# Second attention of a four-layer network: score banks 3 to 4, first-pass banks 4 to 3, and two heads' matmuls issued in turn

## The chip, the cores and the metric

One core of a Trainium2 chip. The time is that of one execution on the device, in microseconds (us). PE is TensorE, DVE VectorE, ACT ScalarE, POOL GpSimd, SP SyncE.

## The reference, cut to what matters

Four layers over x of 2048 tokens with 128 features. Each adds an attention and a feed-forward block to x. The change is in the attention of layer 1, a causal one with 16 heads of 8 features and a relative-position bias:

```python
B, T, C = x.shape                  # in the kernel: 2 sequences of 1024 tokens
qkv = x @ W_attn + b_attn
att = jnp.einsum('bhtd,bhsd->bhts', q, k) * (1.0 / math.sqrt(D)) + rel_bias
att = jnp.where(causal, att, -jnp.inf)
att = jax.nn.softmax(att, axis=-1)
y = jnp.einsum('bhts,bhsd->bhtd', att, v)
return y.transpose(0, 2, 1, 3).reshape(B, T, C) @ W_proj + b_proj
```

## The kernel before

The function `attention_phase` runs twice, for layer 0 and, with `causal` true, for layer 1 (the "second attention", about 507 to 796 us of the trace). 2 x 16 heads make 8 quads of four heads, one turn of the loop each. Every quad is done in two passes.

The **first pass** finds the maximum of each query's scores. Its *units* are a query tile of 128 and up to 512 keys of one head: PE writes the scores to one bank of `mbank` (L821), adds the bias close to the diagonal (L829), and DVE reduces the bank to a negative maximum (L1025) and frees it. 48 units make a quad: 24 pairs, first for the even head (`jj` = 0), then for the odd one (`jj` = 1). Two more uses of the banks are transposes of the maxima ("late" and "turn", L794), which DVE splits into two parts (L1000, L1002); SP sends them back as rows (L560). L1030 combines the maxima once per quad. So 50 uses (`USES`) per quad, taken in turn by the `NM` banks of `mbank`.

The **second pass** goes through 12 groups, key tiles 0 to 3 for the first 512 queries, then 0 to 7 for the second 512; I call them groups 0 to 11. In a group PE writes the four heads' scores, one bank of `ebank` each (L850, three bias parts L859 near the diagonal), ACT takes the exponential (L982) and frees the bank, and PE multiplies all four by the values (L873, 8 matmuls in two passes of float32), one group later. ACT copies the result out (L972). The score banks are `NE`.

A head's operands lie in one half of the partitions: heads 0 and 2 of a quad in rows 0 to 63 of the array, heads 1 and 3 in rows 64 to 127. Each step writes the upper and lower 64 outputs by two matmuls. A plain L850 or L821 step is thus two matmuls of 64 by 64, which use half of the array's rows; the values use all.

PE issues in a fixed order. While quad q's second pass runs, the first pass of quad q + 1 is fed in between: `starts` says which units go with which group. `issue` takes steps of several generators in turn, one `yield` each. The waits that matter:

```python
pe.wait_ge(m_empty, q * USES + (use + 1))   # L812; m_empty starts at NM, +1 per reduction
pe.wait_ge(p_full, step + ...)              # in scores: NE exponentials back
pe.wait_ge(p_full, q * STEPS + (g * QUAD + QUAD + NE))   # in values: all four of the group
```

After the last quad's first pass, eight projection tiles (L429) take banks of `mbank`, one every five uses, and DVE adds them to x (L1092), behind its own work on the next weights.

Of the kernel before, what the change touches and what calls it, by code (L numbers as in the profile page):

```python
# [23 lines left out]
SEQ = 1024  # L24
# [15 lines left out]
NQUAD = BATCH * HEADS // QUAD  # L40
# [423 lines left out]
def attention_phase(nc, S, name, causal, loads=(), weights=None, sort=False):  # L464
# [19 lines left out]
    uses = units[:2] + ["late"] + units[2:18] + ["turn"] + units[18:]  # L484
    USES = len(uses)
    LATE, TURN = uses.index("late"), uses.index("turn")
    NM, WIDE = (4, 512) if causal else (2, SEQ)
    groups = [(h, kt) for h in range(2) for kt in range(4 * h + 4 if causal else BT)]
    lows = [max(kt * P - 512 * h, 0) if causal else 0 for h, kt in groups]
    starts = first_pass_starts(uses, groups, lows, causal)  # L490
    G = len(groups)
    opening = EARLY + starts[len(EARLY):] if causal else starts
    STEPS = QUAD * G
    NE = 3
    BQ = HEADS // QUAD
    layer = 1 if causal else 0
    tiles_from = NQUAD * USES + 1
# [5 lines left out]
    with nc.cleanup_on_exit(), ExitStack() as ctx:  # L503
# [22 lines left out]
        mbank = ctx.enter_context(nc.psum_tensor(f"{name}_mbank", [P, NM, WIDE], F32))  # L526
        ebank = ctx.enter_context(nc.psum_tensor(f"{name}_ebank", [P, NE, 512], F32))

# [37 lines left out]
        def _(sp):  # L566
# [78 lines left out]
            if sort:  # L645
                load_masks()
                sp.wait_ge(bias_parts, 4)
                sp.wait_ge(p_full, NE)
                for copy in range(BATCH):
# [137 lines left out]
        def _(pe):  # L787
            def transpose_maxima(n, units_done, quads_done, h):

                pe.wait_ge(m_empty, max(NM + units_done, n + 1))  # L790
                if quads_done and causal:
                    pe.wait_ge(combined, quads_done)
                bank = n % NM
                nc.tensor.transpose(mbank[0:2 * BT, bank, 0:P], negmax[:, h, :], S.ident[:]).then_inc(m_full, 1)  # L794
# [39 lines left out]
            def scores(q, g, j, buf):  # L834

                h, kt = groups[g]
                s = g * QUAD + j
                pr, jj = j // 2, j % 2
                if kt == 0:
                    pe.wait_ge(rows_loaded[h], q * 64 + 64)  # L840

                step = q * STEPS + s
                pe.wait_ge(p_full, step + (NE if s == 0 and (STEPS - 1) % NE == 0 else 1))
                lo = lows[g]
                rows, mine = slice(64 * jj, 64 * jj + BROWS), slice(64 * jj, 64 * (jj + 1))
                turn = S.anti[mine, 64 * (1 - jj):64 * (2 - jj)]
                near = causal and kt >= 4 * h - 1
                for c in range(P // COLS):
                    at = kt * P + COLS * c
                    last = nc.tensor.matmul(ebank[COLS * c:COLS * (c + 1), s % NE, lo:512],  # L850
                                            S.b_still[rows, buf, pr, at:at + COLS], S.b_moving[rows, buf, h, pr, lo:512],
                                            start=True, stop=not near)
                yield
                for part in range(PARTS if near else 0):
                    for c in range(2):
                        at = kt * P + HALF * c - 512 * h
                        first, end = max(at, 0), min(at + NEARBY, 512)
                        if first < end:
                            last = nc.tensor.matmul(ebank[HALF * c:HALF * (c + 1), s % NE, first:end], turn,  # L859
                                                    bias_b[mine, buf, pr, part, first - at:end - at],  # L860
                                                    start=False, stop=part == PARTS - 1)
                    yield
                last.then_inc(e_full, 1)

            def values(q, g, buf):

                h, kt = groups[g]
                if kt == 0:
                    pe.wait_ge(acc_empty, q * 2 + (h + 1))
                pe.wait_ge(p_full, q * STEPS + (g * QUAD + QUAD + NE))  # L870
                lo = lows[g]
# [6 lines left out]
            def issue(*steps):  # L878
                steps = list(steps)
                while steps:  # L880
                    steps = [s for s in steps if next(s, True) is None]

            def turn(q):

                buf = q % 2
                pe.wait_ge(b_loaded[buf], q // 2 * B_DMA + B_DMA)
                for g in range(G):
                    at = starts if q else opening
                    n, end = q * USES + at[g], q * USES + at[g + 1]
                    middle = (n + end) // 2  # L890
                    if causal:
                        issue(scores(q, g, 0, buf), scores(q, g, 1, buf))
                        issue(first_pass(n, middle))
                        issue(scores(q, g, 2, buf))
                        previous(q, g)
                        issue(scores(q, g, 3, buf))
                        issue(first_pass(middle, end))
                    else:
                        issue(scores(q, g, 0, buf))
                        issue(scores(q, g, 1, buf))  # L900
                        issue(first_pass(n, middle))
                        issue(scores(q, g, 2, buf))
                        previous(q, g)
                        issue(scores(q, g, 3, buf))
                        issue(first_pass(middle, end))

            def previous(q, g):
                if g:
                    values(q, g - 1, q % 2)
                elif q:  # L910
                    values(q - 1, G - 1, (q - 1) % 2)

            def first_pass(n, end):
                for n in range(n, end):
                    if n < NQUAD * USES:
                        yield from a_use(n // USES, n % USES)
                    elif n == NQUAD * USES:
                        transpose_maxima(n, n, NQUAD, 1)
                    elif n >= tiles_from and (n - tiles_from) % tile_every == 0 and (n - tiles_from) // tile_every < BT:
                        projected((n - tiles_from) // tile_every)  # L920
                        yield

            def projected(t):

                n = tiles_from + t
                pe.wait_ge(m_empty, NQUAD * USES + max(t + 2, NM + 1))
                pe.wait_ge(divided, 1)
                project_tile(nc, S, layer, t, mbank[:, n % NM, 0:P]).then_inc(m_full, 1)
# [10 lines left out]
            if sort:  # L939
                for side in range(2):  # L940
                    issue(first_pass(10 * side, 10 * side + 10))
                    bias_rows(side)
            issue(first_pass(20 if sort else 0, opening[0]))
            for q in range(NQUAD):
                turn(q)
            values(NQUAD - 1, G - 1, (NQUAD - 1) % 2)
# [1767 lines left out]
```

## Time and profile before

| | us |
|---|---|
| median of 3 runs | 1042.45 (1040.85 to 1044.25) |
| span of the profiled execution | 1041.8 |
| PE busy | 903.3 (87%) |
| DVE busy | 804.5 (77%) |
| ACT busy | 612.7 (59%) |
| second attention, first to last exponential | 524.6 to 794.4 |

### The profile page before, as it was taken

To read this page: it belongs to the slowest core of one execution; us is meant where nothing else is said; L and a number is where in the kernel's file an instruction comes from. 1 tells how busy PE (TensorE), PEld (TensorE's weight loads), DVE (VectorE), ACT (ScalarE), POOL (GpSimd) and SP (SyncE) were. 2 spreads that over 40 slices of the span, in tenths; PEclk is the share of its full clock that TensorE was granted. 3 is DMA by queue.
4 is the path that set the end of the run, shared out by engine and by line. 5 is a ranking of instruction groups with operands and counts; after the bars stand their busy time and mean duration, and the time that the engine had idled before them with its cause. 6 is when DMAs were issued, how large, how long until landed. Compare 5 with 4: busy or idle time off the path is not lost. (4 is left out here: it accounts for less than half of the span.)

```text
span 1041.8 us, 22164 instructions
## 1 busy us (share of the span) xinstructions
PE 903.3 (87%) x8501; PEld 460.0 (44%) x8501; DVE 804.5 (77%) x1600; ACT 612.7 (59%) x1280; POOL 199.4 (19%) x249
## 2 busy tenths in 40 slices
PE   5589999999999898975689999999989998777788
PEld 3212222222222223873345545555434776645568
DVE  7789999999899861647777878777851677799687
ACT  3228888888888686534146777676653446433552
POOL 2202033341202110540200001103000023123221
PEclk9659999999999899996679999999975998988899
DMA  2632435523426320111645544333100000000001
GB/s 77 189 82 65 113 101 117 117 56 90 110 83 130 116 39 15 53 50 41 191 104 144 151 103 103 86 82 89 42 6 23 12 1 2 1 0 1 4 6 36
DMA packets 62677, 73.71 MB, mean 71 GB/s; under 512 B 21143, under 2 KB 46864, under 8 KB 62558
## 3 DMA queue, kind: packets, MB, share of 16 engines
q1 hardware_dynamic: 48222, 49.23, 19.3%
q0 software_dynamic: 8576, 17.86, 7.0%
q10 hardware_dynamic: 5776, 5.22, 1.6%
q8 instruction: 68, 1.11, 0.5%
q14 instruction: 35, 0.29, 0.1%
HBM read 44.59 MB, written 18.16 MB: 60 GB/s over the span
## 5 line engine op out<-in xcount | busy, mean ns | idle before, releaser
L1025 DVE TENSOR_REDUCE a_negmax<-a_mbank 128x1 f32<-128x1024 f32 (+4 forms) x640 | 488.1, 817 | 73.8 <-PE a_mbank L829 36.0
L982 ACT ACTIVATE a_probs<-a_ebank 128x512 f32<-128x512 f32 (+3 forms) x896 | 436.2, 555 | 171.0 <-PE a_ebank L859 89.9
L850 PE MATMUL a_ebank<-b_moving,b_still 50*128 50x512 bf16 (+4 forms) x1280 | 270.7, 368 | 20.9 <-ACT a_probs L982 11.2
L821 PE MATMUL a_mbank<-a_moving,a_still 48*128 48x512 bf16 (+4 forms) x1280 | 262.8, 376 | 22.7 <-DVE a_negmax L989 10.0
L873 PE MATMUL a_acc<-a_probs,a_slot_v 128*32 128x512 f32 (+3 forms) x1792 | 226.9, 580 | 1.1 <-ACT a_probs L982 1.1
L850 PEld LDWEIGHTS a_ebank<-b_moving,b_still 58*64 58x64 bf16 (+1 forms) x1280 | 85.5, 102 | 257.0 <-ACT a_probs L982 200.6
L821 PEld LDWEIGHTS a_mbank<-a_moving,a_still 56*64 56x64 bf16 (+1 forms) x1280 | 69.0, 104 | 89.7 <-DVE a_negmax L1025 65.3
L859 PE MATMUL a_ebank<-a_bias_b,anti 64*64 64x176 bf16 (+4 forms) x1728 | 89.3, 233 | 0.0
L859 PEld LDWEIGHTS a_ebank<-a_bias_b,anti 64*64 64x64 bf16 x1728 | 70.6, 111 | 9.7 <-issue 1.5
L829 PE MATMUL a_mbank<-bias_a,anti 64*64 64x176 bf16 (+3 forms) x576 | 65.1, 237 | 0.0
L873 PEld LDWEIGHTS a_acc<-a_probs,a_slot_v 128*32 128x32 f32 x1792 | 35.8, 109 | 52.2 <-issue 41.0
L1501 DVE SCALAR_TENSOR_TENSOR x<-m_yp,w,x 128x128 f32<-128x128 f32 x128 | 36.0, 344 | 19.4 <-PE m_yp L1351 19.2
L436 POOL DMA_DIRECT2D sums<-vo x14 | 8.9, 639 | 206.1 <-ACT vo L972 164.9
L1190 ACT ACTIVATE m_hid<-m_hp,m_own 128x128 f32<-128x128 f32 x92 | 26.2, 368 | 27.8 <-PE m_hp L1149 27.8
L1351 PEld LDWEIGHTS m_yp<-w,m_hid 128*128 128x128 f32 x256 | 34.2, 196 | 18.8 <-issue 13.4
L1391 ACT ACTIVATE m_hid<-m_hp,b 128x512 f32<-128x512 f32 x32 | 21.5, 682 | 28.8 <-PE m_hp L1342 28.8
L1262 POOL DMA_INDIRECT spread_rows<-m_y,m_token x23 | 24.6, 1071 | 64.1 <-DVE m_y L1231 64.1
L1351 PE MATMUL m_yp<-w,m_hid 128*128 128x128 f32 x256 | 35.0, 281 | 2.2 <-ACT m_hid L1391 2.0
L1342 PE MATMUL m_hp<-xnT,w 128*128 128x512 f32 x64 | 35.1, 632 | 1.9 <-PEq L2651 1.9
L829 PEld LDWEIGHTS a_mbank<-bias_a,anti 64*64 64x64 bf16 x576 | 34.5, 113 | 2.8 <-issue 0.7
L1092 DVE TENSOR_TENSOR x<-a_mbank,x 128x128 f32<-128x128 f32 x16 | 4.3, 289 | 32.8 <-PE a_mbank L429 32.7
L1149 PE MATMUL m_hp<-m_xT,m_own 128*128 128x128 f32 x184 | 26.7, 291 | 1.6 <-DVE m_xT L1216 0.6
(388 smaller groups left out, 1116.3 us busy)
## 6 DMA issues: line engine op xcount, KB each, us to landing
a_slot_v<-vo SPq DMA_DIRECT2D x16, 512.0 KB
b_moving<-stack SPq DMA_DIRECT2D x64, 96.0 KB
b_still<-stack SPq DMA_DIRECT2D x32, 192.0 KB
a_still<-stack SPq DMA_DIRECT2D x60, 96.0 KB, 2.8
a_moving<-stack SPq DMA_DIRECT2D x60, 96.0 KB, 2.7
expert<-in_expert_rows POOLq DMA_DIRECT2D x8, 578.0 KB, 4.1
a_bias_b<-trow SPq DMA_DIRECT2D x32, 66.0 KB
b_moving<-a_mparts SPq DMA_DIRECT2D x124, 2.0 KB
```

The lines of the kernel that those rows point to most:

```text
L821: last = nc.tensor.matmul(mbank[COLS * c:COLS * (c + 1), bank, lo - left:hi - left], S.a_still[rows, q % 2, pr, at[c]:at[c] + COLS], S.a_m ...
L829: last = nc.tensor.matmul(mbank[COLS * c:COLS * (c + 1), bank, first - left:end - left], turn, bias_a[mine, q % 2, pr, first + shift:end + ...
L850: last = nc.tensor.matmul(ebank[COLS * c:COLS * (c + 1), s % NE, lo:512], S.b_still[rows, buf, pr, at:at + COLS], S.b_moving[rows, buf, h, ...
L859: last = nc.tensor.matmul(ebank[HALF * c:HALF * (c + 1), s % NE, first:end], turn, bias_b[mine, buf, pr, part, first - at:end - at], start ...
L873: last = nc.tensor.matmul(acc[32 * j:32 * (j + 1), lo:512], slot_v[:, buf, j, kt, :], probs[:, g % 2, j, lo:512], start=kt == 0, stop=g + ...
L982: nc.scalar.activation(probs[:, g % 2, j, lows[g]:512], ebank[:, s % NE, lows[g]:512], ACT.Exp).then_inc(p_full, 1)
L1025: nc.vector.tensor_reduce(to[:, at:at + 1], mbank[:, (index - 1) % NM, 0:right - left], AX.X, ALU.max, negate=True).then_inc(m_empty, 2 if ...
L1149: last = nc.tensor.matmul(hp[:, b % 2, m * P:(m + 1) * P], own[:, b % 3, m * P:(m + 1) * P], xT[:, b % 2, :], start=True, stop=True)
L1190: last = nc.scalar.activation(hid[:, b % 2, m, :], hp[:, b % 2, m * P:(m + 1) * P], ACT.Relu, bias=own[:, b % 3, MLP * P + m:MLP * P + m + 1])
L1342: nc.tensor.matmul(hp[:, i % HB, :], w1[:, e, :], S.xnT[:, c * CH:(c + 1) * CH], start=True, stop=True).then_inc(h_full, 1)
L1351: last = nc.tensor.matmul(yp[:, i % 2, t * P:(t + 1) * P], hid[:, i % 2, t * P:(t + 1) * P], w2[:, e, 0, :], start=True, stop=True)
L1501: last = nc.vector.scalar_tensor_tensor(S.x[:, CT * c + t, :], yp[:, i % 2, t * P:(t + 1) * P], w[:, CT * c + t, e:e + 1], S.x[:, CT * c + ...
```

## The change

For the causal attention only, `NM` goes from 4 to 3 banks of `mbank` and `NE` from 3 to 4 banks of `ebank`; the total stays at seven. In each group scores of heads 2 and 3 are issued together, step by step in turn, as heads 0 and 1 were, and ahead of the values of the group before instead of around them. `two_heads` issues two neighbouring units (even and odd head) in turn, and `whole` moves the borders of the groups so that no such pair is cut.

```diff
-    NM, WIDE = (4, 512) if causal else (2, SEQ)
+    NM, WIDE = (3, 512) if causal else (2, SEQ)
...
-    NE = 3
+    NE = 4 if causal else 3
...
                     if causal:
                         issue(scores(q, g, 0, buf), scores(q, g, 1, buf))
-                        issue(first_pass(n, middle))
-                        issue(scores(q, g, 2, buf))
+                        two_heads(whole(n), whole(middle))
+                        issue(scores(q, g, 2, buf), scores(q, g, 3, buf))
                         previous(q, g)
-                        issue(scores(q, g, 3, buf))
-                        issue(first_pass(middle, end))
+                        two_heads(whole(middle), whole(end))
...
+            def head_of_unit(n):
+                use = uses[n % USES]
+                return None if n >= NQUAD * USES or type(use) is str else use[3]
+
+            def whole(n):
+
+                return n + 1 if head_of_unit(n) == 1 else n
+
+            def two_heads(n, end):
+
+                while n < end:
+                    width = 2 if n + 1 < end and head_of_unit(n) == 0 else 1
+                    issue(*(first_pass(m, m + 1) for m in range(n, n + width)))
+                    n += width
...
-            issue(first_pass(20 if sort else 0, opening[0]))
+            if causal:
+                two_heads(0, whole(opening[0]))
+            else:
+                issue(first_pass(20, opening[0]))
```

What this moves on PE, first around group 6. These are PE's rows of the kernel before, from head 3's scores of group 5 (first row) to the values issued in group 6 (last row); x2 is one step of one head.

```order
L850 MATMUL a_ebank<-b_moving,b_still 64x512 x2
L821 MATMUL a_mbank<-a_moving,a_still 64x128 x2
L829 MATMUL a_mbank<-bias_a,anti 64x64
L829 MATMUL a_mbank<-bias_a,anti 64x128
L821 MATMUL a_mbank<-a_moving,a_still 64x512 x4
L850 MATMUL a_ebank<-b_moving,b_still 64x512 x4
L821 MATMUL a_mbank<-a_moving,a_still 64x256 x2
L829 MATMUL a_mbank<-bias_a,anti 64x176 x2
L821 MATMUL a_mbank<-a_moving,a_still 64x256 x2
L829 MATMUL a_mbank<-bias_a,anti 64x176 x2
L850 MATMUL a_ebank<-b_moving,b_still 64x512 x2
L873 MATMUL a_acc<-a_probs,a_slot_v 32x512 x4
```

The same place in the changed kernel, from the last units of group 5 to the units behind group 6's values:

```order
L821 MATMUL a_mbank<-a_moving,a_still 64x512 x4
L850 MATMUL a_ebank<-b_moving,b_still 64x512 x4
L821 MATMUL a_mbank<-a_moving,a_still 64x256 x4
L829 MATMUL a_mbank<-bias_a,anti 64x176 x4
L850 MATMUL a_ebank<-b_moving,b_still 64x512 x4
L873 MATMUL a_acc<-a_probs,a_slot_v 32x512 x4
L821 MATMUL a_mbank<-a_moving,a_still 64x512 x4
L821 MATMUL a_mbank<-a_moving,a_still 64x384 x4
L829 MATMUL a_mbank<-bias_a,anti 64x176 x4
```

Every unit now stands beside its twin (x4), the twin's L821 and its wait stand ahead of the first unit's bias L829, and all four scores stand ahead of the values.

The second place is the last quad's second pass, where only scores, values and projection tiles are left. PE before, from tile 3's group (the first row is the scores of group 4) to tile 5:

```order
L850 MATMUL a_ebank<-b_moving,b_still 64x512 x6
L873 MATMUL a_acc<-a_probs,a_slot_v 32x128 x4
L850 MATMUL a_ebank<-b_moving,b_still 64x512 x2
L429 MATMUL a_mbank<-heads_out,vo 128x128
L850 MATMUL a_ebank<-b_moving,b_still 64x512 x6
L873 MATMUL a_acc<-a_probs,a_slot_v 32x512 x4
L850 MATMUL a_ebank<-b_moving,b_still 64x512 x2
L429 MATMUL a_mbank<-heads_out,vo 128x128
```

And PE in the changed kernel, the same stretch:

```order
L850 MATMUL a_ebank<-b_moving,b_still 64x512 x8
L873 MATMUL a_acc<-a_probs,a_slot_v 32x128 x4
L429 MATMUL a_mbank<-heads_out,vo 128x128
L850 MATMUL a_ebank<-b_moving,b_still 64x512 x8
L873 MATMUL a_acc<-a_probs,a_slot_v 32x512 x4
L429 MATMUL a_mbank<-heads_out,vo 128x128
```

The scores of head 3 (x2) moved from between values and tile to ahead of the values; the tiles keep their groups.

## Rows read from the trace of the kernel before

**Rows 1.** The page, busy us, share of the span and instructions.
```profile
PE 903.3 (87%) x8501; PEld 460.0 (44%) x8501; DVE 804.5 (77%) x1600; ACT 612.7 (59%) x1280; POOL 199.4 (19%) x249
```

**Rows 2.** Line L1030: ns min/median/max, first and last start in us.
```profile
L1030 DVE TENSOR_TENSOR a_negmax<-a_negmax x8: 174/176/176, 534.4 to 751.4; 128x16 f32<-128x16 f32 x8
```

**Rows 3.** Windows: length, busy PE, PEld, DVE, ACT, POOL, granted clock, DMA, GB/s.
```profile
658.70:689.40 30.70, 29.34 (x578) 15.85 (x578) 24.58 (x53) 21.75 (x51) 2.62 (x5) 1.00 0.38 88
507.50:522.80 15.30, 12.76 (x109) 5.19 (x105) 15.01 (x34) 0.49 (x1) 3.73 (x1) 0.50 0.83 259
540.20:547.00 6.80, 6.80 (x60) 2.08 (x55) 3.77 (x9) 4.24 (x8) 0.00 (x0) 0.50 1.03 228
764.90:768.50 3.60, 0.10 (x2) 0.00 (x0) 3.43 (x7) 0.60 (x1) 0.00 (x0) 1.00 0.00 0
```

**Rows 4.** Waits of PE and DVE, 658.7 to 689.4: us, times, longest.
```profile
PE a_mbank L794 <- DVE a_negmax L1030: 0.7, 1, 0.7
PE a_mbank L794 <- DVE a_negmax L1025: 0.5, 1, 0.5
...
DVE a_negmax L1025 <- PE a_mbank L829: 4.3, 5, 1.3
DVE a_negmax L1025 <- PE a_mbank L821: 1.4, 3, 0.8
```

**Rows 5.** Lines by form, DVE, the same stretch: busy us, mean ns, idle before.
```profile
L1025 DVE TENSOR_REDUCE a_negmax<-a_mbank 128x1 f32<-128x512 f32 x24 | 15.2, 682 | 1.4 <-PE a_mbank L821 1.4
```

**Rows 6.** Timeline of DVE: start us, us of the merged run, xcount.
```profile
668.98 1.28 DVE L1025 TENSOR_REDUCE a_negmax<-a_mbank 128x1 f32<-128x512 f32 x2
...
658.82 0.48 DVE L1025 TENSOR_REDUCE a_negmax<-a_mbank 128x1 f32<-128x128 f32 x2
```

**Rows 7.** Timeline of PE behind head 3's scores of group 5.
```profile
670.79 0.44 PE L821 MATMUL a_mbank<-a_moving,a_still 56*64 56x512 bf16 x4
...
671.07 0.22 PE L829 MATMUL a_mbank<-bias_a,anti 64*64 64x64 bf16 x2
```

**Rows 8.** Timeline of PE in group 1, 384 columns.
```profile
659.25 0.36 PE L850 MATMUL a_ebank<-b_moving,b_still 58*64 58x384 bf16 x4
...
659.66 0.28 PE L821 MATMUL a_mbank<-a_moving,a_still 56*64 56x256 bf16 x4
...
659.85 0.33 PE L850 MATMUL a_ebank<-b_moving,b_still 58*64 58x384 bf16 x2
```

**Rows 9.** Timeline of PE around the values of group 6.
```profile
671.87 0.40 PE L850 MATMUL a_ebank<-b_moving,b_still 58*64 58x512 bf16 x2
672.20 1.06 PE L873 MATMUL a_acc<-a_probs,a_slot_v 128*32 128x512 f32 x8
...
673.20 0.61 PE L821 MATMUL a_mbank<-a_moving,a_still 56*64 56x512 bf16 x6
```

**Rows 10.** Timeline of DVE after the unit of 673.20.
```profile
673.69 1.75 DVE L1025 TENSOR_REDUCE a_negmax<-a_mbank 128x1 f32<-128x512 f32 x3 [0.21 <-PE a_mbank L821]
```

**Rows 11.** Timeline of all engines around one wait for a bank.
```profile
612.25 1.29 DVE L1025 TENSOR_REDUCE a_negmax<-a_mbank 128x1 f32<-128x512 f32 x2 [0.21 <-PE a_mbank L821]
...
612.99 0.10 PEld L821 LDWEIGHTS a_mbank<-a_moving,a_still 56*64 56x64 bf16 x2 [0.29 <-DVE a_negmax L1025]
613.00 0.40 PE L821 MATMUL a_mbank<-a_moving,a_still 56*64 56x512 bf16 x2
...
613.24 0.38 PE L850 MATMUL a_ebank<-b_moving,b_still 58*64 58x512 bf16 x2
```

**Rows 12.** Timeline of all engines at tile 4 of the last quad.
```profile
768.17 0.88 DVE L1092 TENSOR_TENSOR x<-a_mbank,x 128x128 f32<-128x128 f32 x4
...
768.51 0.49 PE L429 MATMUL a_mbank<-heads_out,vo 128*128 128x128 f32 x2 [3.51 <-DVE x L1092]
```

**Rows 13.** Timeline of PE in the last quad, at a clock of 0.50.
```profile
776.49 0.63 PE L850 MATMUL a_ebank<-b_moving,b_still 58*64 58x512 bf16 x2
...
777.33 0.79 PE L429 MATMUL a_mbank<-heads_out,vo 128*128 128x128 f32 x2
```

## The prediction

> **What bounds the kernel now.** The page's busy shares come first [rows 1]: PE 87%, DVE 77%, ACT 59%. They average many stages, so I cut the second attention out. L1030 runs once per quad, when the quad's first pass is done: 8 times from 534.4 to 751.4 us [rows 2], so an interval is 31.0 us in the mean, and the undisturbed one from 658.70 to 689.40 is 30.7 [rows 3]. In that stretch PE is marked busy for 29.3 us, DVE for 24.6, ACT for 21.8. PE waits 0.7 + 0.5 = 1.2 us for DVE, DVE waits 4.3 + 1.4 = 5.7 for PE [rows 4]. So PE bounds the quad and DVE is second, at about 25 us: no gain on PE can bring a quad below that.
>
> Two constants of DVE are needed later. A reduction of 512 columns takes 0.68 us [rows 5], but two take 1.28, so the next starts after 0.60; two of 128 take 0.48 [rows 6], so 0.28 long with a pitch of 0.20. Between the two I divide evenly: pitches 0.47 and 0.34 for 384 and 256 columns, lengths 0.55 and 0.42.
>
> **What is gained on PE.** A head uses one half of the array's rows. The obvious reading is that a step of one head leaves the other half idle. The trace says that part of this is used already. In the program the 128-column unit and its bias stand ahead of the 512-column units (the order is shown with the change), yet a 512-column L821 starts at 670.79 and the bias L829 of the 128-column unit only at 671.07 [rows 7]. Matmuls of different heads overtake each other. So I don't subtract idle halves; I add PE's steps up anew, with both heads at once:
> - Two heads' scores: with three bias parts at 384 columns, 659.25 to 659.66 = 0.41; a pair of units of 256 with bias, 659.66 to 659.85 = 0.19 [rows 8]; a plain step of 512, 613.00 to 613.24 = 0.24 [rows 11]. Scaled by columns, scores cost 0.45, 0.40, 0.34, 0.24 near the diagonal, 0.24 far from it and 0.34 at key tile 3, whose bias is short; two such pairs in each of 12 groups make 7.8 us. Units cost 0.30, 0.24, 0.18, 0.12 with bias (512 to 128 columns) and 0.24 without; 24 pairs make 5.3.
> - Values: 672.20 to 673.20 = 1.00, and the change-over ahead of it is 672.20 - 671.87 - 0.24 = 0.09 [rows 9], so 1.08 for 512 columns; two passes of 128 columns at 2.4 GHz are 0.11 and both heads' rows are needed, so each tile less takes 0.21 off. Six of 512 and two of each other width make 10.4.
> - Two transposes: 0.6.
> The sum is 24.1 us if PE never waits, against 30.7 - 1.2 = 29.5 now: **5.4 us to be had per quad**. ACT is no obstacle: with four score banks a head's scores wait for the exponential of the same head one group earlier, and ACT has 21.8 us of work in a quad. The copy L972 moves behind the values and still has a group's time.
>
> A page of the Trainium skill speaks against the overtaking: "TensorE: Matmul & The Clock Gate", Part 3, keeps matmuls in strict program order and lets only weight loads be pulled ahead. By that rule the second scores pair would save 3.9 us and the units half of their 18,432 columns, 3.8, so 7.7 instead of 5.4, and the total below would come to about 1038. Here 670.79 stands before 671.07 against program order, so the measurement decides.
>
> **What is paid: three banks under pairs.** A unit may start when the reduction NM units back is done. With NM = 3 and pairs, the second unit of a pair waits for the first unit of the pair before it. PE waits in order, so behind it stand the first unit's bias (only that releases DVE for this unit), the next scores and the values. The price: a 512-column unit issued at 673.20 [rows 9] is reduced from 673.69 [rows 10], 0.49 later; I use 0.47, and 0.31 after a bias is issued. The reduction lasts 0.68. PE starts 0.06 after its end (612.25 + 0.69 = 612.94, PE at 613.00) [rows 11]. Together 1.21 us from the issue of a pair to the start of the second unit of the next. With one pair of far scores (0.24) and the first pair's own 0.24 between, 0.73 remain as a stall; if the next pair follows at once, 0.97.
>
> Group 6 in full, with its start at 0. Scores 0 and 1 to 0.24. Pair of 256 columns: its second unit waits for a 512 reduced from 0.23, so 0.23 + 0.74 = 0.97; first bias 0.98, PE free at 1.15. Scores 2 and 3 to 1.39, values to 2.47. Pair of 512 to 2.71, reduced from 2.94 and 3.54; DVE was out of work since 2.11. Pair of 384 at once behind it: its second unit waits for 2.94 + 0.74 = 3.68, PE is free at 3.92. Length 3.92 us, of which 1.70 stalls (0.73 and 0.97). I walked all 12 groups so, each with the units that the order gives it. Lengths: 3.24, 3.42, 1.67, 1.32, 3.20, 3.18, 3.92, 2.77, 3.71, 2.48, 1.79, 1.38, together **32.1 us**. The stalls: in group 0 0.52 and 0.75 (the transpose, for L1030), in 1 0.82, in 4 0.47 and 0.96, in 5 0.95, in 6 0.73 and 0.97, in 7 0.47, in 8 0.51 and 0.56, and 0.3 of small ones: 8.0, and 24.1 + 8.0 = 32.1. Groups 2, 3, 10 and 11 hold one pair and no stall; DVE starves there and during values, for some 7.5 us in all.
>
> So the bank taken from the first pass costs 8.0 where 1.2 stood, interleaving gives 5.4: +1.4 us per quad, and with the 7 intervals of [rows 2] **+9.5**.
>
> **Opening and tail.** In the opening DVE is busy for 15.0 of 15.3 us at the lower clock [rows 3]. With three banks it gets gaps of 0.2 to 0.3 us after each narrow pair, some of them hidden behind the first scores' wait for their rows. Bounds 0 and +3; taken **+1**, nearer the hidden end. In the tail the projection tiles (L429) share the first pass's banks. Now tile 4 waits 3.5 us, to 768.51, for L1092, which starts at 768.17 behind DVE's other work [rows 12]. With three banks tile 3 waits, one group earlier, for the same L1092. That group's work, until now done before the wait, lands behind it, where the clock is 0.50: two pairs of scores 0.9, values 2.1, a tile 0.6, so 3.6. In return head 3's scores no longer stand alone between values and tile. One such step took 776.49 to 777.33 = 0.84 [rows 13]; with bias twice and without once that is about 2.1. Net **+1.5**.
>
> **The sum.** 9.5 + 1 + 1.5 = +12. The profiled span is 1041.8 and the median of the runs 1042.45; the difference goes on the latter: **1054.5 us**.
>
> **Rivals.**
> 1. *The stalls are much smaller and overlap pays* (chance 0.2). Half of 8.0: a quad takes 28.1, 7 x -2.6 = -18, with +2.5 at the ends about 1027. None: DVE's 25 bounds, 7 x -5.7 = -40, about 1005. It decides where stalls are under 5.8 us, that is 29.9 per quad. For it: PE waits only 1.2 now, and unit biases may get through earlier than I think. Against it: the 1.21 is from rows, and when a pair starts only one reduction can be pending.
> 2. *A wash* (0.12): stalls of 5.8 to 6.7 us, 1039.4 to 1045.6.
> 3. *The forecast, and the clock falls too* (0.1). PE's granted clock was 1.00 in the idle 764.90 to 768.50 and 0.50 after it; it was 0.50 (the 1.2 GHz level) from 540.20 to 547.00 as well [rows 3]. In group 6 PE would stream under half the time. One such fall of 6.8 us per quad takes up to 3.4 us; half of it 7 times is +12, so 1066. Against it: PE's pauses here stay under 1 us.
> 4. *As worked out* (0.58): stalls of 7 to 9 us, 1047 to 1062, this case's own range.
> The skill's rule on order has a chance of 0.05 within rival 1, at its own 1038.
>
> The range starts at 1036, which leaves out about 0.15 of the fast side, and ends at 1068, beyond rival 3's middle. A measurement of this kernel can tell 0.3%, 3.1 us, from no change: faster 0.2, same 0.12, slower 0.68.
>
> **What would show it.** L1030 at intervals of 32.1. PE's L821 waits for DVE's L1025 for 6 or 7 us per quad, 0.5 to 1.0 each, at the second unit of a pair; PE busy falls to 24 or 25 us. DVE waits some 7.5. Group 6 takes 3.9, groups 3 and 11 under 1.5. In the tail tile 3 waits about 7 us for L1092. Intervals of 26 to 28 would prove the step on the banks wrong, a clock of 0.5 inside the quads speaks for rival 3. The walk is most open where DVE starts after a bias: 0.1 us off there, eleven times, is 1.1 us per quad.

## The result, and the profile after

| | before | after |
|---|---|---|
| median, us | 1041.65 (4 runs, 1035.93 to 1044.25) | 1057.21 (4 runs, 1055.23 to 1059.65) |
| ratio | | 1.019 (95% interval 1.0148 to 1.0232) |
| span of the profiled execution | 1041.8 | 1055.4 |

The change makes the kernel 1.9% slower; the forecast was 1054.5. The before column has one run more than the three that the forecast started from. The page of the changed kernel, to set beside [rows 1]: busy us, share of the span, instructions.

```profile
PE 896.5 (85%) x8501; PEld 439.9 (42%) x8501; DVE 808.0 (77%) x1600; ACT 606.9 (58%) x1280; POOL 199.9 (19%) x249
```

The page alone says almost nothing: PE is busy 7 us less and the span is 14 us longer. Where the time went is seen by cutting at the line that closes a quad's first pass (L1047 now; L1030 in [rows 2]).

```profile
L1047 DVE TENSOR_TENSOR a_negmax<-a_negmax x8: 176/176/177, 538.4 to 774.2; 128x16 f32<-128x16 f32 x8
```

The first closes 4.0 us later than before, and the seven intervals take 235.8 us for 217.0. Windows of the changed kernel, with the columns of [rows 3]: two quads, then the opening, the tail, and two stretches of the tail.

```profile
675.90:708.20 32.30, 28.54 (x578) 13.57 (x578) 24.84 (x53) 21.11 (x51) 2.62 (x5) 1.00 0.35 84
640.10:675.90 35.80, 32.51 (x578) 14.67 (x578) 24.96 (x53) 21.13 (x51) 2.63 (x5) 0.86 0.35 76
...
507.50:538.40 30.90, 25.48 (x301) 11.81 (x297) 24.37 (x51) 6.30 (x15) 3.86 (x1) 0.58 0.53 158
774.20:807.50 33.30, 24.94 (x385) 10.89 (x385) 17.32 (x45) 18.55 (x47) 2.63 (x5) 0.80 0.04 6
786.10:796.30 10.20, 4.96 (x28) 1.57 (x28) 5.86 (x14) 2.07 (x4) 0.00 (x0) 0.50 0.00 0
796.30:807.50 11.20, 11.20 (x218) 5.16 (x214) 0.88 (x3) 9.58 (x24) 0.00 (x0) 1.00 0.00 1
```

The quad of 675.90 ran at a granted clock of 1.00 throughout and took 32.3 us for 30.7 [rows 3]. That of 640.10 has the same instructions and took 35.8, with a mean clock of 0.86. Of the kernel before, these are the opening, the tail, and the part of the tail at the lower clock:

```profile
507.50:534.40 26.90, 22.45 (x297) 11.51 (x293) 23.26 (x50) 6.24 (x15) 3.73 (x1) 0.65 0.60 181
751.40:794.40 43.00, 37.30 (x385) 16.51 (x385) 17.19 (x45) 19.59 (x46) 2.62 (x5) 0.70 0.03 5
768.90:794.40 25.50, 25.41 (x223) 10.62 (x222) 1.31 (x5) 10.41 (x23) 0.00 (x0) 0.50 0.00 1
```

The 13.6 us between the two spans are then made up as follows:

| term | forecast | measured |
|---|---|---|
| seven quads at full clock | +9.5 | 7 x 1.6 = +11.2 |
| the rest of the seven quads, mostly a lower clock | (rival 3) | 18.8 - 11.2 = +7.6 |
| opening | +1 | +4.0 |
| tail | +1.5 | 33.3 - 43.0 = -9.7 |
| all else | 0 | +0.5 |
| sum | +12 | +13.6 |

The -9.7 is taken against one execution of the kernel before, whose tail was unusually long; the part on the tail below returns to it.

The waits of the changed kernel in the quad of 675.90 (us, times, longest):

```profile
PEld a_mbank L821 <- DVE a_negmax L1042: 13.7, 22, 1.1
...
DVE a_negmax L1042 <- PE a_mbank L829: 3.9, 6, 1.0
DVE a_negmax L1042 <- PE a_mbank L821: 3.1, 4, 1.1
PE a_mbank L821 <- DVE a_negmax L1042: 2.7, 7, 0.6
```

The same wait for a bank is marked on two rows, PE's own and that of its weight load (PEld), and they differ: 2.7 us on the one and 13.7 on the other. Group 6 in the next quad shows a single one, with the timeline's columns (start us, us of the merged run, what, and in brackets the idle time ahead and what ended it):

```profile
721.64 0.39 PE L850 MATMUL a_ebank<-b_moving,b_still 58*64 58x512 bf16 x4
...
721.85 1.95 DVE L1042 TENSOR_REDUCE a_negmax<-a_mbank 128x1 f32<-128x512 f32 x4 [0.19 <-PE a_mbank L821]
721.86 0.27 PE L821 MATMUL a_mbank<-a_moving,a_still 56*64 56x256 bf16 x2
...
722.59 0.30 PE L821 MATMUL a_mbank<-a_moving,a_still 56*64 56x256 bf16 x2 [0.46 <-DVE a_negmax L1042]
722.60 0.26 PE L829 MATMUL a_mbank<-bias_a,anti 64*64 64x176 bf16 x2
...
722.70 0.38 PE L850 MATMUL a_ebank<-b_moving,b_still 58*64 58x512 bf16 x2
722.73 0.24 PE L829 MATMUL a_mbank<-bias_a,anti 64*64 64x176 bf16 x2
...
723.11 1.07 PE L873 MATMUL a_acc<-a_probs,a_slot_v 128*32 128x512 f32 x8
...
724.11 0.14 PEld L821 LDWEIGHTS a_mbank<-a_moving,a_still 56*64 56x64 bf16 x6 [0.84 <-DVE a_negmax L1042]
724.11 0.57 PE L821 MATMUL a_mbank<-a_moving,a_still 56*64 56x512 bf16 x6
...
724.56 1.29 DVE L1042 TENSOR_REDUCE a_negmax<-a_mbank 128x1 f32<-128x512 f32 x2 [0.76 <-PE a_mbank L821]
...
725.30 0.11 PEld L821 LDWEIGHTS a_mbank<-a_moving,a_still 56*64 56x64 bf16 x2 [1.05 <-DVE a_negmax L1042]
725.30 0.35 PE L821 MATMUL a_mbank<-a_moving,a_still 56*64 56x384 bf16 x2 [0.62 <-DVE a_negmax L1042]
```

The pair of 256 columns starts its first unit at 721.86 and its second at 722.59, when the reduction of 721.85 has run its 0.68 us. The first unit's bias, which alone can release DVE for it, follows at 722.60. The pair of 512 starts at 724.11, and the second unit of the pair behind it at 725.30: 1.19 us from issue to release, where I had built up 1.21.

Neither mark gives the price of the waits. At 724.11 the weight load is marked as having waited 0.84 us, yet PE came straight from the values (723.11 + 1.07), so this wait cost nothing. At 725.30 PE itself is marked as waiting only 0.62, since the matmul ahead counts as busy to its modelled end. The price is read from the interval between two marks of the program.

### The profile page after: what moved, and what is told of

It reads as the page before. It is cut to its first block and busy times, and to the rows that moved or that the text cites. A ratio compares the mean times of both kernels' runs of the same rounds, so it can differ in the third digit from the quotient of the medians.

```text
span 1055.4 us, 22164 instructions
## 1 busy us (share of the span) xinstructions
PE 896.5 (85%) x8501; PEld 439.9 (42%) x8501; DVE 808.0 (77%) x1600; ACT 606.9 (58%) x1280; POOL 199.9 (19%) x249
## 5 line engine op out<-in xcount | busy, mean ns | idle before, releaser
L999 ACT ACTIVATE a_probs<-a_ebank 128x512 f32<-128x512 f32 (+3 forms) x896 | 431.0, 554 | 188.9 <-PE a_ebank L859 94.2
L821 PE MATMUL a_mbank<-a_moving,a_still 48*128 48x512 bf16 (+4 forms) x1280 | 265.5, 390 | 46.6 <-DVE a_negmax L1042 30.1
L850 PE MATMUL a_ebank<-b_moving,b_still 50*128 50x512 bf16 (+4 forms) x1280 | 242.2, 369 | 16.8 <-ACT a_probs L999 9.7
L850 PEld LDWEIGHTS a_ebank<-b_moving,b_still 58*64 58x64 bf16 (+1 forms) x1280 | 77.5, 104 | 182.3 <-ACT a_probs L999 136.6
L821 PEld LDWEIGHTS a_mbank<-a_moving,a_still 56*64 56x64 bf16 (+1 forms) x1280 | 64.5, 104 | 198.2 <-DVE a_negmax L1042 156.3
L859 PE MATMUL a_ebank<-a_bias_b,anti 64*64 64x176 bf16 (+3 forms) x1728 | 65.1, 230 | 0.0
L873 PEld LDWEIGHTS a_acc<-a_probs,a_slot_v 128*32 128x32 f32 x1792 | 35.8, 109 | 53.4 <-issue 40.7
L859 PEld LDWEIGHTS a_ebank<-a_bias_b,anti 64*64 64x64 bf16 x1728 | 54.5, 111 | 5.7 <-issue 0.4
L829 PE MATMUL a_mbank<-bias_a,anti 64*64 64x176 bf16 (+2 forms) x576 | 53.6, 249 | 0.0
L1207 ACT ACTIVATE m_hid<-m_hp,m_own 128x128 f32<-128x128 f32 x92 | 26.3, 368 | 28.2 <-PE m_hp L1166 28.2
L1109 DVE TENSOR_TENSOR x<-a_mbank,x 128x128 f32<-128x128 f32 x16 | 4.4, 290 | 29.2 <-PE a_mbank L429 29.1
L681 POOL DMA_INDIRECT sorted_rows<-xr,slot x16 | 15.5, 972 | 55.3 <-PE a_mbank L821 55.3
```

What stands on the lines that cost most here:

```text
L821: last = nc.tensor.matmul(mbank[COLS * c:COLS * (c + 1), bank, lo - left:hi - left], S.a_still[rows, q % 2, pr, at[c]:at[c] + COLS], S.a_m ...
L829: last = nc.tensor.matmul(mbank[COLS * c:COLS * (c + 1), bank, first - left:end - left], turn, bias_a[mine, q % 2, pr, first + shift:end + ...
L873: last = nc.tensor.matmul(acc[32 * j:32 * (j + 1), lo:512], slot_v[:, buf, j, kt, :], probs[:, g % 2, j, lo:512], start=kt == 0, stop=g + ...
L999: nc.scalar.activation(probs[:, g % 2, j, lows[g]:512], ebank[:, s % NE, lows[g]:512], ACT.Exp).then_inc(p_full, 1)
L1207: last = nc.scalar.activation(hid[:, b % 2, m, :], hp[:, b % 2, m * P:(m + 1) * P], ACT.Relu, bias=own[:, b % 3, MLP * P + m:MLP * P + m + 1])
```

## The experiments

The quads are compared by one quad of each kernel at a clock of 1.00, a window's length to 0.1 us. Two or more such quads of a profile agree to 0.1 us where they have the same work, so that differences of 1 us stand out clearly. Medians are set against the kernel before on the same chip.

| kernel | first-pass / score banks | scores of heads 2, 3 | units | quad, us | median (before) | ratio, 95% interval |
|---|---|---|---|---|---|---|
| before | 4 / 3 | around the values | single | 30.7 | | |
| e3 | 4 / 3 | around the values | paired | 31.2 | 1038.31 (1036.67) | 1.0015 (0.9995 to 1.0035) |
| e12 | 4 / 3 | paired | single | 33.5 | 1063.62, one run (1037.04) | |
| e1 | 4 / 3 | paired | paired | 33.9 | 1057.53 (1036.67) | 1.0185 (1.0147 to 1.0223) |
| e2 | 3 / 4 | around the values | single | 32.2 | 1052.73 (1036.67) | 1.0145 (1.0114 to 1.0177) |
| e8 | 3 / 4 | paired | single | 31.1 | 1041.29 (1036.53) | 1.0044 (1.002 to 1.0067) |
| after | 3 / 4 | paired | paired | 32.3 | 1057.21 (1041.65) | 1.019 (1.0148 to 1.0232) |
| e7 | 3 / 4 | paired | paired, behind all scores | 30.8 | 1041.18 (1036.53) | 1.0034 (1.0006 to 1.0062) |
| e9 | 3 / 4 | paired | single, behind all scores | 29.8 | 1036.72 (1037.04) | 0.9991 (0.9967 to 1.0015) |

**Banks and order apart.** e1 keeps the new order and takes the banks back; e2 keeps the old order and takes the new banks.

```diff
-    NM, WIDE = (3, 512) if causal else (2, SEQ)
+    NM, WIDE = (4, 512) if causal else (2, SEQ)
-    NE = 4 if causal else 3
+    NE = 3 if causal else 3
```

> The new issue order with the banks of before (4 first-pass, 3 score). Theory (three first-pass banks under pairs make the stalls): PE's waits for the bank reductions fall from about 8 to under 1.5 us per quad, but with three score banks the scores of head 3 need the exponential of head 0 of the same group, issued 0.5 to 0.9 us before and released about 1.2 us after its issue: 0.3 to 0.7 us in most groups, so an undisturbed quad of 30 to 31.3 us, between before (30.7) and after (32.3); time within 1040 to 1050. Rival (the new order itself costs, whatever the banks): 32 us or more per quad, 1055 or more. Second rival (the order pays as soon as the banks are back): 26 to 28 us per quad, under 1020.

```diff
-    NM, WIDE = (4, 512) if causal else (2, SEQ)
+    NM, WIDE = (3, 512) if causal else (2, SEQ)
-    NE = 3
+    NE = 4 if causal else 3
```

> The issue order of before with the new banks (3 first-pass, 4 score). Theory (banks): each unit waits for the reduction three units back, of which the two last are still pending when PE arrives behind the values; stalls of 0.4 to 1.0 us per group, quad 31.5 to 32.5 us, 1050 to 1058. Rival (the order costs, not the banks): 30.7 us per quad and 1042, since only the banks change. If the fourth score bank helps by itself it would show as a quad under 30.7.

The new banks alone cost 1.5 us per quad (32.2 for 30.7), as e2's expectation had it. The new order on the new banks adds 0.1. On the old banks it is worse than anything else, 33.9. The waits of e1 from 669.3 to 703.2, and a piece of its timeline, say why:

```profile
PEld a_mbank L821 <- DVE a_negmax L1042: 5.5, 9, 0.8
PEld a_ebank L850 <- ACT a_probs L999: 4.8, 8, 0.7
PE a_ebank L850 <- ACT a_probs L999: 3.5, 10, 0.4
```

```profile
677.91 0.38 PE L850 MATMUL a_ebank<-b_moving,b_still 58*64 58x512 bf16 x2
677.93 1.57 ACT L999 ACTIVATE a_probs<-a_ebank 128x512 f32<-128x512 f32 x3 [0.74 <-PE a_ebank L850]
...
678.67 0.40 PE L850 MATMUL a_ebank<-b_moving,b_still 58*64 58x512 bf16 x2 [0.38 <-ACT a_probs L999]
679.01 0.43 PE L873 MATMUL a_acc<-a_probs,a_slot_v 128*32 128x128 f32 x8
```

With three score banks and all four heads' scores ahead of the values, head 3 needs the bank of head 0 of its own group. Head 0's exponential starts only at 677.93 and head 3's scores at 678.67, and the values stand behind them. I had expected this wait to be small and the quad at 30 to 31.3; that was wrong by more than 2.6 us. The quad and the time that came, 33.9 and 1057.53, are those of the rival (32 or more, 1055 or more). Its reason, that the order costs whatever the banks, is answered by e8 below: with four score banks the pairs of scores gain. The fourth score bank is thus a condition of this order and not a gain for itself.

**One half of the order at a time, on the old banks.** e3 pairs only the units; e12 pairs only the scores.

```diff
                         two_heads(whole(n), whole(middle))
-                        issue(scores(q, g, 2, buf), scores(q, g, 3, buf))
+                        issue(scores(q, g, 2, buf))
                         previous(q, g)
+                        issue(scores(q, g, 3, buf))
                         two_heads(whole(middle), whole(end))
```

> Banks of before (4 and 3), scores issued as before, only the first-pass units of two heads in turn, with whole pairs per group. Theory: no bank stalls and both halves of the array evenly loaded between two blocks of values, so a quad of 29.7 to 30.5 us and 1034 to 1041. Rival (pairs themselves hold back the first unit's bias and starve VectorE): 31 us or more per quad.

```diff
-                        two_heads(whole(n), whole(middle))
+                        issue(first_pass(n, middle))
                         issue(scores(q, g, 2, buf), scores(q, g, 3, buf))
                         previous(q, g)
-                        two_heads(whole(middle), whole(end))
+                        issue(first_pass(middle, end))
...
-                two_heads(0, whole(opening[0]))
+                issue(first_pass(0, opening[0]))
```

(Both edits are shown against the changed kernel; the banks are those of e1.)

> Old banks (4 first-pass, 3 score), scores in the new order, units one head after the other. Theory (three score banks under two pairs of scores make head 3 wait for the exponential of head 0 of its own group): 33 to 34 us per quad as in e1, with TensorE's L850 waiting for ScalarE 3 us or more. Rival (it was the pairs of units in e1): 31 us or less.

Pairs of units alone gain nothing even with four banks: 31.2 against 30.7, where I expected 29.7 to 30.5. The time, 1038.31, can't be told from before's. Pairs of scores alone give 33.5, with PE's L850 waiting 3.3 us for ACT, both as expected, so e1's loss is theirs. (e12's single time is above e1's median; three of its seven quads, those of 34.8, 35.0 and 35.0 us, hold a fall of the clock.)

**The same on the new banks.** e8 has e12's order with three and four banks. e7 moves the first units of a group behind all four scores; e9 does this too, with single units.

> New banks (3 first-pass, 4 score), scores issued in the new order, first-pass units one head after the other as before. Theory: a unit's bias is no longer held back by its twin's wait and VectorE gets it sooner, but both heads do not share the step; with the first effect about the size of the second, 31.3 to 32.3 us per quad. Rival (units in pairs are the whole cost): 30.5 us or less.

```diff
                         issue(scores(q, g, 0, buf), scores(q, g, 1, buf))
-                        two_heads(whole(n), whole(middle))
                         issue(scores(q, g, 2, buf), scores(q, g, 3, buf))
+                        two_heads(whole(n), whole(middle))
                         previous(q, g)
```

> The changed kernel with all four scores of a group ahead of the first group of units: scores 0 to 3, units, values, units. The distance from the units behind the values to the next units grows by one pair of scores, 0.24 to 0.45 us, and the stall there shrinks by that. Theory (bank release): seven stalls of 0.2 to 0.95 us shrink by 2.3 us in all, so a quad of 30.0 to 30.6 us, at or under before's 30.7; time 1030 to 1042. Rival (scores so close together now wait for ScalarE, since four banks are asked for at once): 32 us or more.

```diff
                         issue(scores(q, g, 0, buf), scores(q, g, 1, buf))
+                        issue(scores(q, g, 2, buf), scores(q, g, 3, buf))
                         issue(first_pass(n, middle))
-                        issue(scores(q, g, 2, buf))
                         previous(q, g)
-                        issue(scores(q, g, 3, buf))
                         issue(first_pass(middle, end))
```

(e9's edit on the kernel before; its banks are those of e2.)

> New banks (3 first-pass, 4 score). Scores 0 to 3 of a group first, then units, values, units, the units one head after the other. The kernels with units in pairs behind the scores took 30.85 us per quad, single units between the pairs of scores 31.05. Theory: distance between units and an undelayed bias add up, each worth 0.5 to 1.2 us against the changed kernel: 29.8 to 30.5 us per quad, under before's 30.7; 1028 to 1038. Rival (both only shift the same wait for VectorE's release): 30.8 us or more.

Windows of one quad in e8, in e7 and in e9:

```profile
663.00:694.10 31.10, 28.88 (x578) 14.55 (x578) 24.73 (x54) 21.23 (x51) 2.62 (x5) 1.00 0.36 87
```

```profile
664.90:695.70 30.80, 27.81 (x578) 13.30 (x578) 24.87 (x53) 20.70 (x52) 2.63 (x5) 1.00 0.36 88
```

```profile
663.50:693.30 29.80, 28.12 (x578) 14.33 (x578) 24.89 (x53) 20.61 (x51) 2.58 (x5) 1.00 0.39 91
```

Read against the table these separate the parts. Pairing the scores gains 1.1 (32.2 to 31.1). Pairing the units costs 1.2 (31.1 to 32.3) and again 1.0 (29.8 to 30.8). Moving the first units behind the scores gains 1.3 to 1.5. The quads expected for e7 (30.0 to 30.6) and e8 (31.3 to 32.3) were missed by 0.2 each; e9's, 29.8 to 30.5, was met. e9 is the only order whose quad beats before's, by 0.9 us, yet its time is the same as before's. Its opening closes at 537.1, 2.7 later than before's, and its second interval took 33.5 for 31.9:

```profile
569.00:602.50 33.50, 30.69 (x578) 15.33 (x578) 25.02 (x53) 20.57 (x51) 2.50 (x4) 0.90 0.60 155
```

A mean clock of 0.90 stands there; before had 1.00 in its own second interval (565.40 to 597.30). Over all seven intervals e9 took 216.9 us, before 217.0: what the quads at full clock gained was lost in the first three.

**Shorter reductions.** In e5 (on the changed kernel) and e6 (on the kernel before) DVE reduces only the first 128 columns of each unit, so the maxima leave the other columns out. Both have one run.

```diff
-mbank[:, (index - 1) % NM, 0:right - left],
+mbank[:, (index - 1) % NM, 0:min(right - left, 128) if causal else right - left],
```

> The changed kernel, with every first-pass reduction of the second attention over 128 columns only (the other columns' maxima are left out, so the shift inside the exponentials is another one); matmuls, waits, banks and order stay. A 512-column reduction falls from 0.68 to about 0.28 us. Theory (TensorE stands because a bank comes back 1.2 us after its pair was issued): the release comes 0.4 earlier at ten of the eleven stalls, so a quad falls from 32.3 to 27.5 to 29 us. Rival (what the change costs is issue and change-over time on TensorE, not waiting): 31.5 us or more.

> The same edit on the kernel before. Theory: TensorE waits for reductions only 1.2 us per quad there, so 30.7 falls to 29.5 to 30.3 us; this is then what the old order costs TensorE by itself, to be held against the changed kernel's with the same reductions. Rival: VectorE matters more than the waits show, and it falls below 29.

e5 took 1014.80 and e6 1030.52, against 1036.53. A quad of e5, and a quad of e6:

```profile
643.80:672.20 28.40, 27.43 (x582) 13.56 (x581) 12.79 (x53) 20.53 (x51) 2.62 (x5) 1.00 0.41 96
```

```profile
654.60:683.80 29.20, 28.88 (x586) 15.80 (x578) 12.62 (x54) 21.63 (x51) 2.63 (x5) 1.00 0.38 94
```

The changed kernel gains 3.9 us per quad from reductions that release their banks sooner, the kernel before 1.5 (its quad of 29.2 was expected at 29.5 to 30.3). The release is what the new order waits for, and without most of its length the new order would win by 0.8. My walk has eleven stalls in a quad, each holding one reduction; at 0.68 - 0.28 = 0.40 us less, that is at most 4.4, less where the unit is narrow, so 3.9 fits it. By the walk about 4 us of stalls then remain in e5, from the time between issue and DVE's start (some 0.47) that no short reduction takes away; no run isolates them.

**The wait of the projection tiles.** e4 is the kernel before with DVE's additions of tiles 0 to 3 (one loop before, behind all work on the next weights) taken in between that work, two ahead of each of its two halves.

```diff
                 for i in range(2):
+                    add_tiles(2 * i, 2 * i + 2)
...
-            for t in range(BT):
+            add_tiles(4 if weights is not None else 0, BT)
```

> The kernel before, with the adds of projection tiles 0 to 3 placed among VectorE's quantisation work of the last quad, two ahead of each half. Theory on the tail: TensorE's wait of 3.5 us at tile 4 goes, and with it the clock's fall, which cost 26.6 us at the lower clock before; last exponential 30 to 36 us after the last L1030 row in place of 43.0, total 1030 to 1036. Rival (the clock falls anyway in the tail): only the wait goes, 1038 to 1040.

It took 1033.98 for 1036.67, ratio 0.995 (0.9917 to 0.9982), and its quad stayed at 30.7. Its tail:

```profile
751.90:786.70 34.80, 33.26 (x385) 14.87 (x385) 17.21 (x45) 19.66 (x46) 2.63 (x5) 0.75 0.04 6
```

This is 8.2 us less than the 43.0 of before's profile, but the edit did not give it. e3 leaves the additions where they were and issues the same tail on PE, and its tail was as long as e4's (the second row is its part at the lower clock):

```profile
754.40:789.20 34.80, 33.22 (x385) 14.87 (x385) 17.21 (x45) 19.75 (x46) 2.62 (x5) 0.75 0.04 6
756.60:773.70 17.10, 17.05 (x149) 6.85 (x139) 14.46 (x34) 8.28 (x20) 1.99 (x4) 0.50 0.05 9
```

The first four additions and tile 4 in e3:

```profile
771.21 0.88 DVE L1110 TENSOR_TENSOR x<-a_mbank,x 128x128 f32<-128x128 f32 x4
...
774.03 0.49 PE L429 MATMUL a_mbank<-heads_out,vo 128*128 128x128 f32 x2
```

In e3 and e4 the clock stood at 0.50 for 17.1 us early in the tail. PE was slower on its way to tile 4, which came at 774.03 in e3, and the additions had begun at 771.21, so nothing waited. In before's profile the clock was at 1.00 up to the wait of 3.5 us and at 0.50 for 25.5 us afterwards. With the old banks the edit's own worth is thus known only from the medians, 2.7 us. The tail (expected at 30 to 36 us) and the time (1030 to 1036) were met, but not the theory that the fall of the clock goes with the wait.

e10 and e11 put the same edit on e9 and e7.

> The kernel of e9 with the adds of tiles 0 to 3 placed among the quantisation work, as in e4. Theory: quads as in e9, and the tail from the last combined row to the last exponential at 29 to 31 us instead of 33, since the wait of some 7 us at tile 3 goes: 3 to 5 us less than e9, 1025 to 1034. Rival (the clock's fall decides the tail, and it falls in the opening of the tail anyway): as e9 within 2 us.

> Units in pairs behind the scores (e7) with the early adds. Theory: quads of 30.85 us as in e7, tail 2 to 4 us shorter than its 32.7: 1035 to 1039. It is to be held against e10 on the same chip: if single units are better, e10 is some 3 us faster or more.

e10 took 1030.16 for 1037.04, ratio 0.9914 (0.9879 to 0.9948); it beats both kernels. e11 took 1031.27, ratio 0.9943 (0.9915 to 0.9971). Here the edit pays. On the same chip e10 is 6.6 us under e9, and e11 is 9.9 under e7's median of another chip. The tail of e10, then that of e11:

```profile
751.60:778.30 26.70, 25.01 (x385) 11.02 (x385) 17.13 (x45) 17.90 (x46) 2.60 (x5) 0.87 0.05 8
```

```profile
756.90:780.60 23.70, 21.98 (x385) 10.24 (x385) 16.96 (x46) 18.25 (x46) 2.64 (x5) 1.00 0.05 9
```

Without the edit the tails of e9 and e7 took 33.6 and 32.7 us, with waits of 7.4 and 8.9 for the addition. The tails became shorter by 6.9 and 9.0, the length of the wait. e10 and e11 have the same 385 matmuls in the same order and no wait for an addition. What separates 26.7 from 23.7 is the clock, 0.87 and 1.00, and PE's busy time differs by 3.0.

Both tails are shorter than expected (29 to 31 for e10, 2 to 4 under e7's for e11), and e11's time lies 3.7 us under its range of 1035 to 1039. I had expected e10 to be 3 us faster than e11 or more. In the two profiles e10's last quad closes 5.3 us earlier, but its tail, at the lower clock, is 3.0 longer; the medians differ by 1.1.

## Why the prediction was right, step by step

**The walk of the quad held.** Forecast 32.1, measured 32.3; group 6 forecast 3.92, measured 3.77 (from 721.64 to the next group's scores at 725.41). The other groups, each from its first scores to the next group's, took 3.26, 3.29, 1.88, 1.33, 2.97, 3.43, then behind group 6 2.97, 3.47, 2.72, 1.83 and 1.36 in the quad from 673.19 to 705.47. None is more than 0.25 off the walk, and groups 3 and 11 are under 1.5 as forecast. The step that paid for it, "three banks under pairs", is shown: the timeline has the second unit of each pair starting right behind a reduction, and e5 takes away half of the price by the reduction's length alone.

**The split into 5.4 gained and 8.0 paid came out as a sum, but no run shows either term whole.** Part of the gain is seen directly: groups 2, 3, 10 and 11, which have no stall in the walk, took 6.4 us together for 7.9 before, where the walk had 6.2. Half of the price is shown by e5. Giving the banks back does not yield the 5.4. e1 showed the reverse, because with the old banks a different wait takes over (head 3 on head 0's exponential), and e3 showed that pairs of units lose 0.5 even with four banks. On the new banks, pairs of scores gain 1.1 and pairs of units cost 1.2, so interleaving both costs 0.1 net. "PE never waits" was not reached by any kernel; the shortest quad, e5's, has PE busy for 27.43 of 28.4.

**The overlap of separate steps.** Had single steps not overlapped, the second pair of scores would have been worth 3.9 us. It was worth 1.1 on the new banks (e2 to e8), and the total of 1038 that went with it was missed by 19. This fits the overlap that [rows 7] show, though e8 also moves waits, so it is no measurement of the overlap by itself. The changed kernel shows it too: the scores of 722.70 started ahead of the bias of 722.73, which stands before them in the program. By the Trainium skill, "TensorE: Matmul & The Clock Gate", Part 3, matmuls start in strict program order; these rows disagree.

**Signs.** I wrote that PE's L821 would wait 6 to 7 us and PE's busy time fall to 24 or 25; they were 2.7 and 28.5. The interval was right and these two marks were not: PE counts as busy to the modelled end of its last matmul, so part of each wait hides there. DVE's waits, forecast at 7.5, were 3.9 + 3.1. One sum was off as well: 7 times +1.4 is +9.8, where I wrote +9.5.

**Rival 3 came true in part.** The clock fell to 0.50 in five of the seven quads (3.4 to 13.7 us at a time). With what else made them longer this is +7.6 us, where rival 3 had +12. Against it I had written that the pauses stay under 1 us. PE's own waits were 0.6 at most in the quad of 640.10, which held a fall of 10.2 us, so short pauses were no protection. It isn't settled what starts a fall: e1's quads leave PE idle for more (33.9 - 28.7 = 5.2 us, for 32.3 - 28.5 = 3.8) and all but the first ran at 1.00, and the changed kernel's own quads, alike in their instructions, had 1.00 and 0.86.

**Opening: mis-sized.** Forecast +1 with a bound of +3, measured +4.0. The opening of the changed kernel, waits up to 538.4:

```profile
PEld a_mbank L821 <- DVE a_negmax L1042: 14.1, 26, 1.0
...
PE a_mbank L821 <- DVE a_negmax L1042: 5.0, 15, 0.6
```

The same line in before's opening was 6.0 us on the weight load in 18 waits. DVE is idle for 30.9 - 24.4 = 6.5 us, before 26.9 - 23.3 = 3.6: 2.9 of the 4.0 are gaps on DVE, at my upper bound. The experiments say whose they are. From the opening's first reduction to its close the kernel before took 26.8 us and the changed kernel 30.7. Pairs on four banks took 27.3 (e1) and 26.3 (e3), single units on three banks 27.1 to 29.1 (e8, e9, e2), and pairs on three banks 30.9 once more (e7). So pairs alone cost at most 0.5 and three banks alone 0.3 to 2.3, and the whole comes only with both. What part the mean clock has, 0.58 for 0.65, was not tried.

**Tail: right wait, wrong clock.** Tile 3 did wait for the addition, at the forecast length of 7:

```profile
783.57 0.43 PE L873 MATMUL a_acc<-a_probs,a_slot_v 128*32 128x128 f32 x8
791.34 0.80 PE L429 MATMUL a_mbank<-heads_out,vo 128*128 128x128 f32 x2 [7.35 <-DVE x L1109]
```

The step that failed is "lands behind it, where the clock is 0.50". The clock was at 0.50 from 786.10, half of that inside the wait where it cost nothing, and back at 1.00 from 796.30, so the last 11.2 us ran at full speed; before had 0.50 for 25.5 us to the end of its tail. The tail became 9.7 shorter instead of 1.5 longer. I know of no step in the change that makes the clock recover sooner, and most of the 9.7 belongs to that one execution of before. Beside the experiments the kernel before had medians of 1036.5 to 1037.0, under this profile's span of 1041.8, and e3, which issues before's tail on PE, took 34.8 us for it. Against that tail the changed kernel's is 1.5 shorter: the wait grew from nothing to 7.35, and the time at 0.50 fell from 17.1 us to 13.6, of which 5.2 lie in the wait.

So it is luck that the total came within 3 us. Against the profile of before, +7.6 of clock and +3 of opening cancel against -11.2 of tail. With e3's tail in place of before's, the difference between the spans would be some 21.8 us instead of 13.6 (an estimate), against a forecast of +12. The quads, which decide the sign, were worked out right, and +9.5 of them stands against +11.2 at full clock.

## What to carry to other kernels

Before two streams are interleaved in program order, count the buffers that each pair holds at once: a pair asks for its second buffer before its first unit is complete, so with three banks it stands still for a reduction at eleven places of a quad in the walk, 8.0 us in all. Change the order and the buffers separately, since here each is a condition of the other and neither alone shows what the two give. What paid was to place independent work between a producer and the wait that needs it (single units behind all scores, 0.9 us per quad at full clock, though only together with the early additions did it show in the time) and to move a late consumer's small additions ahead of its big work, where tiles waited 7 to 9 us for them. Before a gain is read off two profiles, look for a third kernel with the same stretch: e3 showed that 8.2 us in a tail were not the edit's.

## What the runs showed of the hardware

The granted clock moves a stretch's time with nothing changed in its program. The tails of e10 and e11 have the same 385 matmuls in the same order: 26.7 us at a mean clock of 0.87, 23.7 at 1.00. The tails of before and of e3 do as well: 43.0 at 0.70, with a wait of 3.5, and 34.8 at 0.75. Two quads of the changed kernel with the same instructions took 32.3 at 1.00 and 35.8 at 0.86. In e4 no tile waits for its addition, and the clock still stood at 0.50 for 17.1 us, so a wait for the addition is not what makes it fall there.

The waits for first-pass banks of one quad read 13.7 us on the weight loads and 2.7 on the matmuls, and the walk puts all stalls at 8.0. The first counts waits beside PE's work, the second leaves out what a modelled end covers. The interval between two marks of the program is the number to believe.

Steps of different heads start out of program order: 722.70 ahead of 722.73 in the changed kernel, as in [rows 7].
